# Shifted rows of x loaded from memory, offset matmuls in two halves, and a new order at both ends of an eight-image convolution chain

## What is computed

```python
x = x + L0(_gn(x))    # depthwise 3x3, then 3 channel mixes (softmax(att), pointwise, softmax(glob))
x = x + L1(_gn(x))
# L1: off = conv3x3(y, w_off) (2 values per pixel and channel); every pixel of y is
#     read at (row + off0, col + off1) with bilinear weights; conv3x3(mapped, w_conv) + b
```

## Time and profile before

| | |
|---|---|
| median of 3 runs | 766.88 us (766.66 to 767.16) |
| the profiled execution, its own time | 767.21 us |
| its span, first to last instruction | 765.3 us |
| busy: TensorE, VectorE, GpSimd, ScalarE | 712.4, 538.9, 489.4, 471.6 us |
| mean granted TensorE clock | 0.98 of full speed |

### The profile page before, as it was taken

The page is one execution under the profiler, slowest core; times in us unless marked ns, Lnnn a source line. Parts: engine busy times, 40 slices in busy tenths (PEclk is TensorE's granted clock), DMA queues, the critical chain, the costliest instruction groups (busy, mean ns, idle before and its releaser), DMA issues. The chain is left out here.

```text
span 765.3 us, 9619 instructions
## 1 busy us (share of the span) xinstructions
PE 712.4 (93%) x2876; PEld 282.9 (37%) x2876; DVE 538.9 (70%) x1111; ACT 471.6 (62%) x821; POOL 489.4 (64%) x432
## 2 busy tenths in 40 slices
PE   4799975999999999999999999999999999999956
PEld 4343322333433333433434333333433334334312
DVE  3686698458985699567986499766996586557632
ACT  7477874675557646667556764765556755686520
POOL 4014965874768654966748665877548748699840
PEclk9999986999999999999999999999999999999979
DMA  8939615499549896798849897597948563757455
GB/s 144 201 73 164 150 40 129 104 153 184 118 120 225 141 216 120 167 192 167 176 108 229 137 216 149 140 213 146 215 97 195 114 137 63 161 106 181 114 139 130
DMA packets 216138, 114.29 MB, mean 149 GB/s; under 512 B 142768, under 2 KB 208400, under 8 KB 212496
## 3 DMA queue, kind: packets, MB, share of 16 engines
q1 hardware_dynamic: 192048, 101.83, 64.4%
q10 hardware_dynamic: 24032, 11.78, 8.7%
HBM read 16.91 MB, written 16.78 MB: 44 GB/s over the span
## 5 line engine op out<-in xcount | busy, mean ns | idle before, releaser
L1274 DVE COPY_PREDICATED other_row<-down_ps,row_diff 128x768 f32<-128x768 int32 x128 | 124.2, 1025 | 144.8 <-ACT down_ps L897 144.8
L693 PE MATMUL off_ps<-x1a,wo 128*128 128x512 f32 x384 | 185.1, 619 | 12.3 <-DVE other_row L1286 6.3
L1080 POOL TENSOR_TENSOR other_row<-other_row,x_quads 128x512 f32<-128x512 f32 x64 | 76.0, 1187 | 180.4 <-DVE other_row L1286 180.4
L693 PE MATMUL off_ps<-x1b,wo 128*128 128x512 f32 x384 | 175.2, 592 | 0.0
L586 PE MATMUL c_ps<-xb,w 128*64 128x512 f32 x336 | 153.0, 605 | 9.1 <-DMA xb<-xa 9.1
L586 PE MATMUL c_ps<-mapb,w 128*64 128x512 f32 x336 | 153.8, 598 | 5.7 <-DVE x1a L1258 5.7
L588 PE MATMUL c_ps<-xa,w 128*64 128x512 f32 x336 | 153.0, 605 | 0.0
L886 ACT ACTIVATE other_row<-row_diff 128x768 f32<-128x768 f32 x128 | 101.6, 841 | 81.1 <-POOL row_diff L1066 70.9
L588 PE MATMUL c_ps<-mapa,w 128*64 128x512 f32 x294 | 134.4, 598 | 0.0
L693 PEld LDWEIGHTS off_ps<-x1a,wo 128*128 128x128 f32 x384 | 69.0, 192 | 115.3 <-issue 100.2
L693 PEld LDWEIGHTS off_ps<-x1b,wo 128*128 128x128 f32 x384 | 72.6, 189 | 92.2 <-issue 92.2
(11 more groups left out here) (128 smaller groups left out, 970.9 us busy)
## 6 DMA issues: line engine op xcount, KB each, us to landing
x1b<-x1a SPq DMA_DIRECT2D x28, 520.0 KB, 6.5
mapb<-mapa SPq DMA_DIRECT2D x28, 520.0 KB, 8.1
mapa<-mapped SPq DMA_DIRECT2D x224, 64.0 KB, 2.1
xb<-xa SPq DMA_DIRECT2D x26, 520.0 KB, 10.1
out_dram<-x1a SPq DMA_DIRECT2D x49, 256.0 KB, 4.7
x_quads<-x1a SPq DMA_DIRECT2D x192, 65.0 KB, 2.5
xa<-in_x_dram ACTq DMA_DIRECT2D x40, 256.0 KB, 6.4
xa<-in_x_dram SPq DMA_DIRECT2D x16, 256.0 KB, 6.9
```

Source lines behind the costliest of these rows:

```text
L693: last = nc.tensor.matmul(off_ps[k % 2][:, CH * n:CH * n + CH], wo[wpar][:, kx, :], rows[:, 4 * k:4 * k + 4, kx:kx + W], start=(kx == 0), ...
L1080: step(pool.tensor_tensor(split(column), split(column), own, ALU.add))
L1274: last = dve.copy_predicated(other_row[n][:, :, KR // 2 * odd:KR // 2 * odd + KR // 2, :], bass.AP(tensor=rows.tensor, offset=rows.offset ...
```

## The change

- **xb from memory.** `copy_xb` becomes `load_xb`: four DMAs for a half image straight out of x in memory, with no wait for xa. `pad_x` waits for these.
- **Offsets in two halves.** Each 128-column matmul of `offsets` becomes two of 64 columns, into partitions 0 to 63 and 64 to 127.
- **Biases.** The three horizontal taps of w1, wo and w2 are summed once (`w1_sum`, `wo_sum`, `w2_sum`) and each `norm` is followed by mean x rstd (`scaled_x`, `scaled_1`), so that `b1`, `bo` and `b2` need two one-column matmuls in place of six (`bo`: three).
- **norm.** It works on a pair (mean, half variance), spread once; the root is iterated on all 128 partitions in two steps in place of three, and the last four copies go. Copies of 32-partition pieces are now `tensor_scalar` with a column of ones. One more small product (`scaled_...`) and one more wait follow.
- **Order in image 0.** The norm of x of image 2 moves from chunk 5 to chunk 3, its `b1` and `pad_x` from chunk 7 to 4, its first three conv1 groups from image 1 to chunks 5, 6 and 7 of image 0; `bo` of image 1 and its first `pad_x1` go from behind chunk 7 to chunk 6.
- **The end.** Part 1 (chunks 4 and 5 of the last image) is no longer moved by DMA: ScalarE copies 20 pieces and VectorE 12, each 32x256. VectorE does its 12 behind the last `deform`, ahead of the left-over conv2 read-outs. Chunks 6 and 7 are shared out as before.

```diff
+    FIRST_FURTHER = [[], [], [], [], [], [0], [1], [2]]
+    SECOND_CONV1 = [[3], [4, 5], [6, 7], [], [], [], [], []]
-    NEXT_BIAS = [7] + [6] * (NB - 1)
+    NEXT_BIAS = [6] * NB
+    FURTHER_BIAS = [4] + [NK - 1] * (NB - 1)
...
+        END_SHARES = [{"act": END_ROWS[:20], "dve": END_ROWS[20:]},
+                      {"dve": END_ROWS[:12], "act": END_ROWS[12:22], "pool": END_ROWS[22:]}]
...
-            def copy_xb(i, half, copied):
+            def load_xb(i, half, loaded):
+                rows = x[i].rearrange("c (b r) w -> c b r w", r=4)
+                to = xb_of(i)
                 b, e = half * HB, half * HB + HB
-                to, rows = xb_of(i), xa_of(i)
-                sp.dma_start(to[0:2 * Q, b + 1:e + 1, :], rows[2 * Q:P, b:e, :]).then_inc(copied[half], DMA)
-                sp.dma_start(to[2 * Q:P, b:e, :], rows[0:2 * Q, b:e, :]).then_inc(copied[half], DMA)
+                for q in range(4):
+                    first = b + 1 if q < 2 else b
+                    sp.dma_start(to[Q * q:Q * q + Q, first:first + HB, 1:W + 1], rows[:, b:e, (q + 2) % 4, :])\
+                      .then_inc(loaded[half], DMA)
...
-                        sp.wait_ge(xa_loaded[half], xa_count(i + 2))
                         sp.wait_ge(conv1_done, 8 * (i + 1) + (5 if half == 0 else 8))
-                        copy_xb(i + 2, half, xb_copied)
+                        load_xb(i + 2, half, xb_loaded)
...
+            def mean_sum(bank, sums, scaled):
+                kinds = sums.shape[1] // 64
+                for t in range(2):
+                    c = 64 * (t % kinds)
+                    last = nc.tensor.matmul(bank[64 * t:64 * t + 64, 0:1], sums[:, c:c + 64], scaled[:, :],
+                                            start=True, stop=True)
...
                     for kx in range(3):
-                        last = nc.tensor.matmul(off_ps[k % 2][:, CH * n:CH * n + CH], wo[wpar][:, kx, :],
-                                                rows[:, 4 * k:4 * k + 4, kx:kx + W], start=(kx == 0), stop=(kx == 2))
+                        for t in range(2):
+                            last = nc.tensor.matmul(off_ps[k % 2][64 * t:64 * t + 64, CH * n:CH * n + CH],
+                                                    wo[wpar][:, kx, 64 * t:64 * t + 64],
+                                                    rows[:, 4 * k:4 * k + 4, kx:kx + W],
+                                                    start=(kx == 0), stop=(kx == 2))
...
                 for q in range(4):
-                    step(dve.tensor_copy(mean[Q * q:Q * q + Q, :], mv[:, 0:1]))
+                    step(dve.tensor_scalar(pair[Q * q:Q * q + Q, :], mv[:, :], ones[0:Q, :], None, ALU.mult))
...
                 for _ in range(3):
                     settle()
-                    step(dve.tensor_scalar(newton[:, :], rs[:, :], rs[:, :], var_eps[:, :], ALU.mult, ALU.mult))
+                    step(dve.tensor_scalar(newton[:, :], rstd[:, :], rstd[:, :], half_var, ALU.mult, ALU.mult))
                     settle()
-                    step(dve.tensor_scalar(newton[:, :], newton[:, :], -0.5, 1.5, ALU.mult, ALU.add))
-                    settle()
-                    step(dve.tensor_scalar(rs[:, :], rs[:, :], newton[:, :], None, ALU.mult))
-                settle()
-                for q in range(4):
-                    step(dve.tensor_copy(rstd[Q * q:Q * q + Q, :], rs[:, :]))
+                    step(dve.tensor_scalar(rstd[:, :], newton[:, :], 1.5, rstd[:, :], ALU.subtract, ALU.mult))
...
-                    if after and k == (4 if i else 3):
+                    if after and k == (4 if i else 1):
                         x_stats(i + 2, 0)
-                    if after and k == 5:
+                    if after and k == (5 if i else 2):
                         x_stats(i + 2, 1)
+                    if after and k == (5 if i else 3):
                         x_norm(i + 2, i % 2)
+            dve.wait_ge(end_pads, 1)
+            copy_end_rows(0)
             for _, i, m in left_over:
                 add_group(i, i % 2, i % 3, m, CONV2_GROUPS[m], bank("c2", i, m))
```

More of the change, by code:

```diff
@@ L606, in first_group @@
                 return last
-            def mean_sum(bank, col, weights, mean):
-                last = None
-                for kx in range(3):
-                    for t in range(2):
-                        last = nc.tensor.matmul(bank[64 * t:64 * t + 64, col:col + 1], weights[:, kx, :], mean[:, :],
-                                                start=(kx == 0), stop=(kx == 2))
+            def mean_sum(bank, sums, scaled):
[4 more added lines that the diff above has]
+                                            start=True, stop=True)
                 return last
@@ L645, in offsets_bias @@
                 pe.wait_ge(wo_ready, i + 1)
-                for kx in range(3):
-                    last = nc.tensor.matmul(ps[:, 0:1], wo[wpar][:, kx, :], mean_1[par][:, :],
-                                            start=(kx == 0), stop=(kx == 2))
-                last.then_inc(bo_summed, 1)
+                mean_sum(ps, wo_sum, scaled_1[par]).then_inc(bo_summed, 1)
             def conv2_bias(i, wpar, par, ps):
                 pe.wait_ge(w2_ready, i + 1)
-                mean_sum(ps, 0, w2[wpar], mean_1[par]).then_inc(b2_summed, 1)
+                mean_sum(ps, w2_sum, scaled_1[par]).then_inc(b2_summed, 1)
             def conv2(i, wpar, m, ps):
@@ L1100, in _ @@
             pool.wait_ge(end_pads, 1)
-            for which in end_rows_by("pool"):
-                to, rows = end_row(*which)
+            for which in END_SHARES[1]["pool"]:
+                to, rows = end_row(*which, 1)
                 last = pool.tensor_copy(to, rows)
-            last.then_inc(end_rows["pool"], 1)
+            last.then_inc(end_rows[1]["pool"], 1)
             pool.wait_ge(is_far_ready, 1)
@@ L1292, in _ @@
                 x_stats(0, half)
+            dve.wait_ge(s_setup["pool"], 2)
             x_norm(0, 0)
@@ L1324, in _, with copy_end_rows @@
                             add_group(i - 1, (i - 1) % 2, (i - 1) % 3, m, CONV2_GROUPS[m], bank("c2", i - 1, m))
-                    if after and k == (4 if i else 3):
+                    if after and k == (4 if i else 1):
                         x_stats(i + 2, 0)
-                    if after and k == 5:
+                    if after and k == (5 if i else 2):
                         x_stats(i + 2, 1)
+                    if after and k == (5 if i else 3):
                         x_norm(i + 2, i % 2)
+            def copy_end_rows(part):
+                dve.wait_ge(mapped_ready, NK * NB - 2 + 2 * part)
+                for which in END_SHARES[part]["dve"]:
+                    to, rows = end_row(*which, part)
+                    p = Q * (2 * which[1] + which[2])
+                    last = dve.tensor_scalar(to, rows, ones[p:p + Q, :], None, ALU.mult)
+                last.then_inc(end_rows[part]["dve"], 1)
+            dve.wait_ge(end_pads, 1)
+            copy_end_rows(0)
             for _, i, m in left_over:
@@ L1333, in _ @@
                 if m == 2:
-                    dve.wait_ge(mapped_ready, NK * NB)
-                    dve.wait_ge(end_pads, 1)
-                    for which in end_rows_by("dve"):
-                        to, rows = end_row(*which)
-                        last = dve.tensor_copy(to, rows)
-                    last.then_inc(end_rows["dve"], 1)
+                    copy_end_rows(1)
                 add_group(NB - 1, (NB - 1) % 2, (NB - 1) % 3, m, END_GROUPS[m], bank("c2", NB - 1, m))
```

174 lines of the change are left out of this document (105 added, 69 removed).

## The result

| | before | after |
|---|---|---|
| median of 9 runs each, side by side | 767.31 us (765.76 to 768.25) | 764.05 us (761.45 to 764.57) |
| ratio | | 0.995, 95% interval 0.9936 to 0.9963 |
| profiled execution, its span | 765.3 us | 759.7 us |
| busy: TensorE, VectorE, GpSimd, ScalarE | 712.4, 538.9, 489.4, 471.6 us | 697.8, 563.6, 490.8, 478.8 us |

The change is 0.5% faster. The forecast was 728.7 us with a range of 708 to 744, so the time lies 35 us above the one and 20 above the other.

What follows compares the result with a forecast made beforehand. TensorE's list was taken to bound images 1 to 6. Terms of -2.2, -4.1, -10.4, -10.8, -3.6 and -7.1 sum to -38.2 us, giving a 727.1 us span and a 728.7 us forecast, range 708 to 744.

Steps and rivals of the forecast that it cites:

- The step that failed: In the two norms of an image: they change by -1.0 and +0.25, so 0.75 us less per image.
- Offsets in halves: In TensorE's offset matmuls: 12 pairs take 5.14 us, 0.35 less per chunk, 2.75 us less per image.
- The wait of TensorE: At the read-out behind both norms: the wait grows from 1.27 to 2.4 us, so a middle image gains 2.7.
- Start and image 0: Up to image 1's first group: 6.3 us earlier, 2.2 of it at the start, with 1.8 charged for the clock.
- Image 1: It loses 7.85 us by three moved groups and 3.85 by the shorter list; its wait grows 1.3: -10.4 us.
- Image 7: Up to its first own conv2 group: paced by SyncE's earlier moves and GpSimd, its length stays, difference 0.
- The end: From image 7's first own conv2 group on: ScalarE and VectorE copy part 1, -7.1 us; VectorE's copying is late next.
- xb from memory: In the loading of xb: worth nothing, with four more issues per image in SyncE's slack.
- The second: Rival on the offset matmuls: the halves keep the pace of 0.446, 12.1 us more, 741 us; chance 0.12.
- the fourth: Rival on the offset matmuls: the two halves do not run together, 330 us more, 1059 us; chance 0.03.
- the third: Rival on image 0's order: the early groups of image 2 give nothing, 7.9 us lost, 736.6 us; chance 0.11.
- the first: Rival on norm and the end: tensor_scalar with a column of ones is free of GpSimd, 709.4 us; chance 0.18.

Runs made afterwards that it cites:

- narrow_whole: narrow_both with the offsets as matmuls of 128 columns again: 741.28 us, 2.0 more than narrow_both.
- narrow_both: The changed kernel with both spreads of norm (four_mv and the pair) as eight one-element-wide copies in place of four 32x2 tensor_scalar: 739.24 us, ratio to before 0.963.
- before_load_xb: The kernel before with only xb loaded from memory by four DMAs per half image, without the wait for xa: 766.95 us, ratio 1.0003.
- after_copy_xb: The changed kernel with xb copied from xa again: 764.75 us against 764.05.
- narrow_old_order: narrow_both with the order of the kernel before in image 0: 743.29 us.
- copy_mv: The changed kernel with the four 32x2 instructions that fill four_mv as tensor_copy again, not tensor_scalar: 755.35 us, 8.7 less than the changed kernel.
- narrow_mv: narrow_both, but the pair of mean and half variance is spread by four tensor_scalar of 32x2: 747.12 us.
- narrow_mv_ts: narrow_both, but the eight 32x1 instructions that fill four_mv are tensor_scalar with ones, not tensor_copy: 742.44 us.
- narrow_xb_act: narrow_both with the loads of xb issued by ScalarE behind chunks 4 and 5, not by SyncE: 740.25 us.
- narrow_late_load: narrow_both with the loads of the second half of xa issued behind chunk 4 and not chunk 3: 748.98 us, 9.7 more.
- before_halves: The kernel before with only the offsets in two halves of 64 columns: 763.41 us, ratio 0.9949.

## Why the prediction was wrong, step by step

**The step that failed** is the price of `norm` and, with it, TensorE's wait for the read-out and the clock behind that wait. The sum had the two norms 0.75 us shorter per image; they came out 1.07 longer, since the `tensor_scalar` of 32x2 go one to an operation of GpSimd. It put the wait at 2.4 us per middle image and no loss of clock behind it. Over images 2 to 5 the waits grew from 5.2 to 16.7 us, 6.8 more than the sum had, and the fallen clock costs 7.4. With 1.8 us that the list shrank less, that is 16.0 of the 17.0 us by which these four images miss.

- **Offsets in halves: right in size, wrong in worth.** 5.15 us per chunk, 5.25 to 5.28 where an edge group follows, in place of 5.35. Image 6, in which TensorE waits for nothing, shows the halves alone: 85.64 us in narrow_whole (552.11 to 637.75) and 83.24 in narrow_both (548.88 to 632.12), 2.4 for eight chunks, 0.30 each. With the biases: a middle image before is 88.10 us with 1.27 of wait, image 3 of narrow_both 85.83 with 2.43, so the list shrank by 3.4 where 3.85 was put.
- **norm: this step failed.** It put two wide copies to an operation of GpSimd and kept that price for `four_mv`, though the change turns these copies into `tensor_scalar`, and the row beside it showed such an instruction ending with GpSimd's operation. The 64 instructions went from 35.0 us busy (547 ns) to 56.5 (883 ns). From the first spread's aggregate to the scaled weights, the norm of x takes 8.59 us in place of 8.93 (term: -1.0), the norm of x1 9.48 in place of 8.07 (term: +0.25): +1.07 per image where -0.75 was put. The pair, which was to cost 1.2 more in the norm of x1, did not meet GpSimd there (0.97 us in both norms; the copies before took 0.66): `four_mv` had waited GpSimd out. The Trainium skill ("SBUF — State Buffer", SBUF: two separate sides) describes an exclusive lock, held for a whole instruction. That agrees with one `tensor_scalar` for one operation of 1.3 us. It does not give the order of service that tells the two forms apart: in the kernel before the four copies from 266.62 take 1.02, 0.16, 1.14 and 0.16 us, so every second one gets in where GpSimd goes from one operation to the next, and in the changed kernel the four from 259.67 take 0.37, 1.32, 1.34 and 1.32.
- **The wait of TensorE: mis-sized with it.** It was to grow to 2.4 us per middle image. In image 2 it is 3.96, and 1.01 more at a second read-out (281.92). Over images 2 to 5 it is 4.2 us in the mean (1.3 before), 1.8 more than put, and 1.8 is also what image 2's norms miss.
- **The clock behind the wait: missing.** The prediction charged a fall of the clock in image 0 and none here. At half clock the group behind the wait takes 1.36 us more in image 2. From the end of the wait to the next offsets it is 4.08, 5.36, 4.41 and 4.40 us in images 2 to 5, and 2.72 in image 1, where the wait is 1.73 us and the clock stays: 7.4 us in four images. So in image 2: waits +3.7, clock +1.4, list -3.4 gives +1.7; measured +1.96 (213.00 to 303.06 against 88.10). The sum had -2.7.
- **Start and image 0: right in form.** The start gave 0.8 us of the 2.2: image 0's offsets begin at 55.93 in place of 56.69. With GpSimd idle the first norm got only 0.35 shorter where 0.9 was put, since a `tensor_scalar` of 32x2 takes 0.22 us there and the copy took 0.16, and it begins 0.3 later; w1 is ready when it was (24.6). In image 0 the wait has moved to `b1`, as predicted, 6.49 us in place of 5.7:

```profile
101.27 0.38 PE L633 MATMUL c_ps<-dve_columns,w_sum 128*64 128x1 f32 x4 [6.49 <-DVE w L1270]
101.47 2.83 PE L715 MATMUL off_ps<-x1a,wo 128*64 128x512 f32 x6
```

  w1 is ready at 101.1 (put: 98.8). 1.5 of these 2.3 us is the later start (the last statistics ahead of the norm run at 89.81, put 88.3), 0.8 the norm, in which `four_mv` took 5.32 us (91.14). The offsets behind it take 8.13 us, 3.0 over 5.15, where 1.8 was charged. These two, 2.3 and 1.2, more than cover the 2.9 us that the stage misses.
- **Image 1: the same two causes.** The three groups did leave the image. But chunk 5's offsets wait 3.63 us for a `deform` behind the norm of x1, run at half clock (7.92 in place of 5.15), and a read-out takes 1.73 more: 8.1 us, of which 1.7 was in the sum.
- **Image 7: a cover that was not there.** The prediction let this stage keep its length, being paced by SyncE and GpSimd. If SyncE paces it, what TensorE has gained by then is lost: SyncE stands where it stood. The first quads of image 7 are issued at 637.50 us, before and after alike (637.31), while TensorE is 3.6 us ahead at 655.00. Before, then after:

```profile
637.31 2.65 SPq L328 DMA_DIRECT2D x_quads<-x1a  x4
```

```profile
637.50 3.05 SPq L349 DMA_DIRECT2D x_quads<-x1a  x4
...
664.54 4.01 SPq L349 DMA_DIRECT2D x_quads<-x1a  x2
```

  They wait for GpSimd's chunk 4 of image 6, behind the norm of x1. The chain that ended last runs through SyncE's issues from there to 691 us. So 3.6 us were given back, and the second quads took 14.0 us (664.54 to 678.56) where they took 11.7 (666.22 to 677.94). narrow_whole and narrow_both show it too: their TensorE starts image 7 at 637.75 and 632.12 and reaches its own conv2 at 703.6 and 702.57.
- **The end: right in size, in part by luck.** 6.3 us of 7.1. The twelve copies of VectorE take 9.1 us, as put. But the prediction let two of them in per operation of GpSimd; as `tensor_scalar` they go one to an operation while that works (1.26 to 1.35 us each) and take 0.42 to 0.44 us each behind it. It is the same mistake as in `norm`, and here it does not show in the sum. TensorE waits for them:

```profile
726.92 1.34 DVE L1385 TENSOR_SCALAR xa<-mapped,ones 32x256 f32<-32x256 f32 x1
728.27 1.35 DVE L1385 TENSOR_SCALAR xb<-mapped,ones 32x256 f32<-32x256 f32 x1
...
734.89 0.79 PE c_ps L606
```

  The last row is of the chain that ended last; the wait ahead of it is 3.83 us.
- **xb from memory: nothing here, right** (before_load_xb, after_copy_xb). That it costs 5.9 us as soon as norm is short was not seen; the prediction looked at SyncE's slack, and not at what else the DMA engines carry.
- **The rivals.** The second (halves at 0.446) and the fourth (halves one after the other) are refuted by the pace; the third (early groups give nothing) by narrow_old_order (4.1 us, measured with the short norm); the first by 883 ns. What happened was none of them: `tensor_scalar` waits more than the copy, not less. The range left it out, since the price was looked for between the copy's and none.

**How far the cause is shown.** That the form and the width of `norm`'s spreads set VectorE's stretch and with it TensorE's wait is shown by copy_mv, narrow_mv, narrow_mv_ts and narrow_both. What the mistake in the price is worth is another number. With `four_mv` in the form that the sum priced (copy_mv) the kernel takes 755.4 us, 8.7 of the 35.3 us by which the forecast missed. Narrow spreads take it to 739.2, 24.8 of the 35.3, but they are a better kernel than the one that was forecast: the sum counted on 3.25 us for `four_mv` in the norm of x, and narrow copies take 0.91. So that the remainder ends near the forecast (730.9 with xb copied and other shares, 2.2 above it) does not show that each term is accounted for. That the clock falls behind the waits, and what it costs, is read from the traces; no run kept the wait and took the fall away. That mapb is made late by other transfers is shown in kind (narrow_xb_act, narrow_late_load); which transfer would have to give way was not found.

## What to carry to other kernels

When an edit swaps one form of instruction for another, price it by the rows of the new form, also where it stands beside a busy neighbour, and look at what comes next: a wait for GpSimd that one instruction no longer takes is taken by the next wide one. A shorter list of the busiest engine is worth only what the second chain lets through, and a longer wait can cost clock on top, so the gain of such an edit can be less than nothing. Find first what the busiest engine waits for at its longest, shorten that, and only then its own list: in this kernel TensorE's list lost some 2.4 us per image by the halves, and the kernel 3.6 us in all with the long norm and 2.0 with the short one.

## What the runs showed of the hardware that was not expected

- A VectorE instruction of 32 partitions with two elements each (SBUF to SBUF) beside GpSimd took 883 ns in the mean as `tensor_scalar` and 547 to 575 as copy; with one element each 130 to 147 ns (copy) and 191 to 209 ns (`tensor_scalar`), with no wait in 128 instructions. Beside GpSimd two narrow copies are cheaper than one wide one; where GpSimd is idle they are not (eight narrow 0.91 us, four wide 0.72).
- Waits of TensorE of 1.87 us left its clock at full speed; of 2.34 and 2.47 us it fell to half from the fourth pair on (before_halves); of 2.73 us it stayed at full in one case (copy_mv, 295.57). Behind 3.96 us it was at half from the first pair in one image (298.98) and from the third in another (478.36, both in the changed kernel). There is no single length from which it falls in these traces.
- The moves of mapa (64 KB) landed 2.1 us after issue in the median, and 6.4 us after the last issue where four loads of 256 KB ran beside them (narrow_both, 246.9 to 253.3).
